# TensorE's order inside the attention units, the first shared projections, and three smaller moves in a Flamingo-style block

## The reference

```python
    x = x + jnp.tanh(g_xattn[0]) * _L0_xattn_ref(_layernorm(x, axis=-1), ctx_1024, ctx_1024, ...)
    x = x + jnp.tanh(g_ffn[0]) * _L0_ffn_ref(_layernorm(x, axis=-1), ...)
# attention: softmax(gamma * Q K^T / 4 + delta * bias) V, then Wo
# feed-forward:
        logits = xf @ gate_w + gate_b
        top_w, top_i = jax.lax.top_k(logits, K)
        for e in range(E):
            h = jax.nn.gelu(xf @ w1[e] + b1[e], approximate=False)
            out = out + combine[:, e:e + 1] * (h @ w2[e] + b2[e])
        shared = jax.nn.gelu(xf @ ws1 + bs1, approximate=False) @ ws2 + bs2
```

## Time and profile before

| what | before |
|---|---|
| median of 3 runs | 480.17 us (478.01 to 481.91) |
| the profiled execution's own time | 479.94 us |
| its span (first to last instruction) | 478.1 us |
| mean granted PE clock | 0.989 |
| PE / PEld busy | 459.8 us (96%) / 391.2 us (82%) |
| DVE / ACT / POOL busy | 357.1 (75%) / 312.7 (65%) / 244.1 us (51%) |
| PE busy, 0 to 24 us | 20.86 of 24 us |
| PE busy, 280 to 460 us | 180 of 180 us |

### The profile page before, as it was taken

One profiled execution on the slowest core, in us unless ns is written; L12 is line 12 of the kernel. 1 busy time (PEld: TensorE's weight loads), 2 busy tenths in 40 slices (PEclk: granted clock), 3 DMA queues, 4 the chain that ended last, 5 costly groups with the idle time before them and its releaser, 6 DMA issues.

```text
span 478.1 us, 17105 instructions
## 1 busy us (share of the span) xinstructions
PE 459.8 (96%) x6326; PEld 391.2 (82%) x6327; DVE 357.1 (75%) x839; ACT 312.7 (65%) x852; POOL 244.1 (51%) x277
## 2 busy tenths in 40 slices
PE   8899989999999989999999999999999999999993
PEld 4566779899999856666668999999999999999992
DVE  5897898999999966898975896566656665666562
ACT  5996788999999986878865753443344334433440
POOL 4689998998745665377850024232223222322332
PEclk9999998999999989999999999999999999999998
DMA  8704456766754377136338353423342332233223
GB/s 316 261 12 106 85 154 182 214 191 184 213 159 122 127 271 303 35 114 201 136 106 200 111 102 45 54 44 55 55 47 44 56 54 44 44 61 49 44 34 35
DMA packets 61443, 55.81 MB, mean 117 GB/s; under 512 B 37712, under 2 KB 51920, under 8 KB 61264
## 3 DMA queue, kind: packets, MB, share of 16 engines
q1 hardware_dynamic: 54240, 45.66, 33.7%
q0 software_dynamic: 7152, 9.44, 11.0%
HBM read 30.94 MB, written 19.03 MB: 105 GB/s over the span
## 4 chain that ended last, share of the span: by engine, by line
PE 69%; ACT 20%; DVE 4%; DMA 3%; issue 2%; POOL 1%; POOLq 0%; DVEq 0%; ACTq 0%
PE banks L1293 34%; PE bank L1293 32%; ACT W L750 10%; ACT W L756 5%; DMA out<-xrow,idu 2%; PE bank L1400 2%; ACT W L764 1%; ACT W L780 1%; ACT W L772 1%; PE banks L1314 1%; DMA W<-ctxT 1%; ACT xT L785 1%; DVE mx L958 0%; DVE W L963 0%; DVE gwhl L1039 0%
## 5 line engine op out<-in xcount | busy, mean ns | idle before, releaser
L886 ACT ACTIVATE hbuf<-banks,b1t 128x128 f32<-128x128 f32 x312 | 88.8, 368 | 113.3 <-PE banks L1293 110.9
L686 POOL DMA_INDIRECT out<-xrow,idu x39 | 61.0, 1564 | 167.8 <-DVE xrow L1266 128.6
L1293 PE MATMUL banks<-xrow,W 128*128 128x128 bf16 x1872 | 110.9, 219 | 0.3 <-issue 0.3
L1293 PEld LDWEIGHTS banks<-xrow,W 128*128 x1872 | 107.3, 98 | 1.8 <-issue 0.6
L1293 PE MATMUL bank<-W,xT 128*128 x936 | 108.4, 273 | 0.0
L1293 PEld LDWEIGHTS bank<-W,xT 128*128 128x128 bf16 x936 | 89.9, 98 | 9.8
L750 ACT ACTIVATE W<-banks,mx 128x128 f32<-128x128 f32 x256 | 69.6, 394 | 2.8 <-DVE mx L958 2.8
L1247 DVE TENSOR_TENSOR xT<-hbuf,xT 128x512 bf16<-128x512 f32 x78 | 54.0, 692 | 2.7
L1245 DVE CAST xT<-hbuf 128x512 bf16<-128x512 f32 x78 | 36.6, 470 | 20.1 <-ACT hbuf L886 19.3
L963 DVE TENSOR_TENSOR W<-bank,W 128x512 bf16<-128x512 f32 x64 | 43.9, 689 | 7.7 <-ACT W L756 4.9
L672 POOL DMA_INDIRECT xs_dram<-W,place x32 | 38.8, 1214 | 17.8 <-DVE W L1180 9.5
(11 more groups left out here) (175 smaller groups left out, 725.4 us busy)
## 6 DMA issues: line engine op xcount, KB each, us to landing
stage<-wts SPq DMA_DIRECT2D x26, 512.0 KB, 4.0
W<-wts SPq DMA_DIRECT2D x10, 512.0 KB, 6.5
xs_dram<-hbuf SPq DMA_DIRECT2D x6, 792.0 KB, 6.2
W<-d_dram SPq DMA_DIRECT2D x32, 128.0 KB, 3.5
W<-ctxT SPq DMA_DIRECT2D x4, 512.0 KB, 5.5
xrow<-x SPq DMA_DIRECT2D x4, 512.0 KB, 7.5
d_dram<-W SPq DMA_DIRECT2D x16, 128.0 KB, 3.9
out<-xrow SPq DMA_DIRECT2D x4, 512.0 KB, 3.5
```

Of the source, the lines that this page charges most:

```text
L686: nc.gpsimd.indirect_dma_start(out, bass.IndirectOffsetOnAxis(idu[:, par, t:t + 1], axis=0), ysb[par][t], None, compute_op=ALU.add).then_i ...
L886: ins = nc.scalar.activation(hbuf[:, q, c * TR:(c + 1) * TR], bank[UPS * par + q][:, c * TR:(c + 1) * TR], ACT.Gelu, bias=b1t[:, par, UC * ...
L1293: return nc.tensor.matmul(o, a, b, start=start, stop=stop, **kw)
```

## The change

Six parts.

1. **Units.** PE's order becomes `weigh_values(2u - 2)`, `turn_probs(2u)`, `weigh_values(2u - 1)`, then in odd units `turn_o`, `turn_probs(2u + 1)`, `turn2`, `gate`, and in even units the first 2 of `project_o`'s 8 matmuls, `turn_probs(2u + 1)`, and the other 6; then `scores(u + 2)`. Neighbours lie in different banks.
2. **Last units.** In units 30 and 31, which have no `scores(u + 2)`, PE does `shared_up(0)` and `shared_up(1)` there. ACT's order behind the units follows: the GELU table, `norm2(13)`, the GELU of step 0, `outputs_high(15)`, `inputs2_high(13)`, then `piece_high` of piece 16; that of piece 17 goes to step m = 3. On POOL `deviation2(14)` comes ahead of piece 16 and piece 17 behind the five shared splits.
3. **Beginning.** The first group's statistics, deviations and norms are made for two sequences at a time, `turn_inputs` takes each sequence as its norm is ready, and it comes after two instead of three parts of `project_values(0)`. ACT's `weight_high(0)` moves behind `norm4(0)`; the low part of the value weights moves from POOL to DVE, the selection rows `selb` from ACT to POOL.
4. **Gate weights.** `split_gate` moves from DVE (unit 3) to POOL, ahead of `clip(0)`.
5. **Last tile.** In step j = 38 PE does half 1 of `up_part(38)` behind both halves of `down_part(37)`.
6. The norms of every group release `turn_inputs` sequence by sequence.

The diff, cut to its core (`ranks`, `w_up`, `shared_up` and others only move up in the file):

```diff
-            def deviation4(g):
-                at = slice(4 * g, 4 * g + 4)
-                pool.wait_ge(ln1_moments, g + 1)
+            def deviation(n, lo, hi):
+                at = slice(lo, hi)
+                pool.wait_ge(ln1_moments, n + 1)
                 link(nc.gpsimd.tensor_tensor(rstd1[:, at], rstd1[:, at], mhalf[:, at], ALU.pow))
...
+            def split_gate():
+
+                gw = col[:, K_GW:K_GW + DC * E].rearrange("p (c e) -> p c e", c=DC)
+                nc.gpsimd.tensor_copy(upb[:], cst[:, C_UP:C_UP + P])
+                link(nc.gpsimd.tensor_copy(gwhl[:, 0], gw))
+                nc.gpsimd.tensor_tensor(gwhl[:, 1], gw, gwhl[:, 0], ALU.subtract).then_inc(gate_split, 1)
+
...
-            pool.wait_ge(w_hi, 2)
-            nc.gpsimd.tensor_tensor(wp_at(2, 1), wst_at(2), wp_at(2, 0), ALU.subtract).then_inc(w_lo[2], 1)
-            deviation4(0)
+            deviation(0, 0, 2)
+            deviation(1, 2, 4)
             pool.wait_ge(ld_cst, 16)
+            nc.gpsimd.tensor_copy(selb.rearrange("p (j t) -> p j t", t=T),
+                                  cst[:, C_SEL:C_SEL + 4 * DC].rearrange("p (j o) -> p j o", o=1).to_broadcast([P, 4 * DC, T])
+                                  ).then_inc(sel_rows, 1)
             nc.gpsimd.tensor_copy(padt[:, :, 3:4], cst[:, C_PAD:C_PAD + TH].rearrange("p (k o) -> p k o", o=1)).then_inc(pad_ready, 1)
-            deviation4(1)
...
-            deviation4(2)
+            deviation(3, 8, 12)
...
+            split_gate()
             clip(0)
             clip(1)
-            deviation4(3)
+            deviation(4, 12, 16)
...
+            deviation2(B - 2)
             piece_low(NOW // 2, 0)
-            deviation2(B - 2)
-            piece_low(NOW // 2, 1)
             deviation2(B - 1)

             for m in range(POOL_SPLITS):
                 pool.wait_ge(sh_hi, m + 1)
                 nc.gpsimd.tensor_tensor(hsplit[:, m % DEEP, 1, :], hbuf[:, m % DEEP, :], hsplit[:, m % DEEP, 0, :],
                                         ALU.subtract).then_inc(sh_ready[0], 1)
+            piece_low(NOW // 2, 1)

             pool.wait_ge(pad_written, PADS)
...
             def norm4(g):
-                act.wait_ge(ln1_rstd, g + 1)
                 if g:
+                    act.wait_ge(ln1_rstd, g + 2)
...
-            nc.scalar.activation(selb.rearrange("p (j t) -> p j t", t=T),
-                                 cst[:, C_SEL:C_SEL + 4 * DC].rearrange("p (j o) -> p j o", o=1).to_broadcast([P, 4 * DC, T]),
-                                 ACT.Copy).then_inc(sel_rows, 1)
+            norm4(0)
             weight_high(0)
-            norm4(0)
             for g in range(Q4):
...
-            act.wait_ge(converted, NOW)
-            piece_high(NOW // 2, 0)
-            act.wait_ge(setup_act, 2)
-            nc.scalar.activation(tgx[:, 1:2], tgf[:, 0:1], ACT.Gelu)
-            norm2(B - 3)
-            piece_high(NOW // 2, 1)
-            outputs_high(B - 1)
-            inputs2_high(B - 3)
...
+            act.wait_ge(setup_act, 2)
+            nc.scalar.activation(tgx[:, 1:2], tgf[:, 0:1], ACT.Gelu)
+            norm2(B - 3)
+            act.wait_ge(pad_written, PADS)
+            gelu_shared(0)
+            outputs_high(B - 1)
+            inputs2_high(B - 3)
+            act.wait_ge(converted, NOW)
+            piece_high(NOW // 2, 0)
...
+                if m == 3:
+                    piece_high(NOW // 2, 1)
...
-                if u == 3:
-                    split_gate()
...
-            statistics4(0)
+            statistics(0, 2)
+            statistics(2, 4)
+            weight_low(2, 1)
...
-            statistics4(1)
+            statistics(4, 8)
...
             def turn_inputs(g):

-                pe.wait_ge(xh_ready, g + 1)
                 if g == 0:
                     pe.wait_ge(ld_cst, 16)
-                    pe.wait_ge(sel_rows, 1)
-                for c in range(DC):
-                    if g:
-                        pe.wait_ge(xT_lo, DC * (g - 1) + c + 1)
-                    for s in range(4):
+                for s in range(4):
+                    pe.wait_ge(xh_ready, 4 * g + s + 1)
+                    for c in range(DC):
+                        if g and s == 0:
+                            pe.wait_ge(xT_lo, DC * (g - 1) + c + 1)
                         ins = nc.tensor.transpose(bank[c][:, s * T:(s + 1) * T], xh[:, s * D + c * P:s * D + (c + 1) * P], ident)
-                    ins.then_inc(xT_ps, 1)
+                        if s == 3:
+                            ins.then_inc(xT_ps, 1)
...
-            def project_o(b):
-                pe.wait_ge(oT_lo, b + 1)
...
-            project_values(0, 0, 3)
+            project_values(0, 0, 2)
             turn_inputs(0)
-            project_values(0, 3, 4)
+            project_values(0, 2, 4)
...
                     weigh_values(2 * u - 2)
+                turn_probs(2 * u)
+                if u >= 1:
                     weigh_values(2 * u - 1)
+                if u % 2 == 1 and b >= 1:
+                    turn_o(b - 1)
+                if u % 2 == 0 and b >= 2:
+                    project_o(b - 2, 0, 1)
+                turn_probs(2 * u + 1)
+                if u % 2 == 0 and b >= 2:
+                    project_o(b - 2, 1, 3)
+                if u % 2 == 1 and b >= 3:
+                    turn2(b - 3)
                 if u % 2 == 1 and b >= 4:
                     gate(b - 4, b - 3)
-                turn_probs(2 * u)
-                if u % 2 == 0 and b >= 2:
-                    project_o(b - 2)
-                if u % 2 == 1 and b >= 1:
-                    turn_o(b - 1)
-                    if b >= 3:
-                        turn2(b - 3)
-                turn_probs(2 * u + 1)
                 if u + 2 < 2 * B:
                     scores(u + 2)
+                else:
+                    piece_converted(pe, 3)
+                    shared_up(u + 2 - 2 * B)
...
-            piece_converted(pe, 3)
-            shared_up(0)
             turn_o(B - 1)
             turn2(B - 3)
-            shared_up(1)
+            shared_up(2)
             project_o(B - 1)
             turn2(B - 2)
-            for m in range(2, AHEAD):
+            for m in range(3, AHEAD):
...
+                last = isinstance(j, int) and j == TILES - 1
+                for q in range(UPS - 1 if last else UPS):
                     up_part(j, par, up_base, q)
                 if not first(j):
                     for q in range(UPS):
                         down_part(j - 1, 1 - par, down_base, q)
+                if last:
+                    up_part(j, par, up_base, UPS - 1)

```

133 lines of the change are left out of this document (69 added, 64 removed).

## The result

The changed kernel took **486.13 us** (median of 4, 485.80 to 486.61) against 479.88 for the kernel before (median of 4, 478.01 to 481.91): ratio **1.0133** (95% interval 1.0096 to 1.0170), 1.3% slower. Repeated on another chip it was 1.0147 (1.0112 to 1.0182). The forecast was 476.0 with a range of 471.5 to 480.5. The profiled execution took 486.42 us with a span of 484.6, 6.5 more than before.

What follows compares the result with a forecast made beforehand. PE was taken as full from 280 to 460 us, with time lost ahead in four places and PE, ACT and DVE near balance in attention. Terms -1.8 - 2.8 - 2.4 + 0.9 + 2.2 = -3.9 gave 476.0 us, range 471.5 to 480.5.

Steps and rivals of the forecast that it cites:

- Units: Attention pairs: ACT's waits for the second turns go, a pair falls from 7.35 to 7.24 us; -1.8 us in all.
- The slower rival: Attention: first turns hold up PE waiting for exponentials, a pair takes 7.95 us, the kernel 485.6 us; chance 0.08.
- Beginning: Program start: queries begin 1.3 us later, partly given back at `turn_inputs(1)`; +0.9 us, bounds 0 and +2.6.
- the clock falls at the beginning: Rival: a 2 us PE hole before the first queries brings the clock down; 477.5 us, chance 0.18.
- Gate weights: Units 4 to 7: moving the split off DVE removes the wait and clock fall; -2.8 us, bounds -3.2 and -1.1.
- What is late next: Behind the gate weights' split on POOL: if its cover goes, `scores(0)` is late next, by under 1 us.
- Last units: Passage to the shared expert: two shared projections fill PE's holes and avoid the half clock; -2.4 us.
- Last tile: End of the kernel: `weigh(37)` and the last adding DMAs come 2.2 us later; +2.2 us, bounds +1.9 and +2.4.
- the third rival: Attention: small PE holes bring the clock down again; 477.7 us, with a second such fall 479.4; chance 0.10.

Runs made afterwards that it cites:

- run 1: Changed kernel with `turn2(b - 3)` again right behind `turn_o(b - 1)` on PE, ahead of the second turns; ratio to the kernel before 1.0032.
- run 2: Changed kernel with ACT's `probs_high(2u + 1)` ahead of `outputs_high(b - 1)` in odd units, PE's order kept; ratio to the kernel before 1.0071.
- run 3: Changed kernel with the whole old order of PE within the units, all else still changed; ratio to the kernel before 1.0071.
- run 12: Kernel before with gate weights, difference loads, last units and late gate products: mended last tile 0.9939; old tile 0.9922; old tile plus changed beginning 0.9977.
- run 7: Kernel before with only the gate weights' split moved to POOL ahead of the first clip; ratio to the kernel before 1.0007.
- run 4: Changed kernel with PE's old order in the last tile; ratio to the kernel before 1.0076.
- run 5: Changed kernel with `weigh(37)` between the splits of the two halves on DVE in the last tile; ratio to the kernel before 1.0090.
- run 11: Kernel before, unchanged, traced again: span 476.6 us; and kernel before with the last-units part, including norms released one by one: ratio 0.9983.
- run 10: Changed kernel with units, beginning and last tile as before, keeping the gate weights and last units; ratio to the kernel before 0.9968.
- run 6: Changed kernel with the old beginning, the rest still changed; ratio to the kernel before 1.0117.

## Why the prediction was wrong

The sum said -3.9 us and the spans differ by +6.5. Of these 10.4 us, 7.8 lie in the term of the units.

**Units (-1.8, measured +6.0): the step that failed.** "The new order lets the second turns start as soon as the exponentials end, so I expect both waits gone." I looked at what the second turns wait for, and not at who waits for what had been moved behind them. `outputs_high(b - 1)` waits, through the bank that both use, for the `turn2(b - 3)` of its own unit. That took 0.66 us of ACT in each odd unit, and ACT was the full engine. Runs 1 and 2 show it from both sides, run 3 prices the order at 0.54 us per pair. The part of the term that I did look at came true: the even unit went from 3.59 to 3.45 us, the 0.14 that I had read as its wait for the second turns. The odd unit, where I had hoped for 0.11, lost 0.69. With that wait mended it still takes 4.13 and 4.17 us (runs 1 and 2), against 3.76 before: smaller waits of ACT are left (0.23 and 0.40), and the order gains nothing there. The slower rival had the size right (7.95 forecast, 7.90 measured) by luck. Its mechanism, PE's wait at the first turns, is real (0.48 us in even units), but the even unit in which it stands got shorter, and run 2 gains 0.28 of a pair with PE's order unchanged.

**Beginning (+0.9, measured +2.6).** The shift of the queries was 1.8 instead of 1.3. The rival "the clock falls at the beginning" (0.18) came true in this trace, and in five of the nine traces with that beginning: behind holes of 2.68, 2.69, 2.83, 2.84 and 2.84 us. In the four others the hole was 2.68. Against a price of 2.1 us (run 12), 0.9 left out too much. The deviation took 1.07 us beside DVE against 0.73, and DVE's L1060 1.00 beside POOL's cast, against 0.35 in the kernel before without it. The first lay on the path, the second in front of a wait. The Trainium skill's rule ("SBUF — State Buffer", the section "Who interferes with whom") that spoke against the move, by which a DVE operation with two SBUF inputs contends with one of POOL that reads SBUF, is borne out. Each lost less than it overlapped, 0.34 of 0.51 us and 0.65 of 0.86.

**Gate weights (-2.8, measured -3.2 in place).** Right in the stretch, and no part of the result: alone it gives nothing that can be measured (run 7, 1.0007). "What is late next" I had sought at `scores(0)`; it was the difference load, three engines off (POOL, SP, then the transfer). In the changed kernel's trace it had cover, because the beginning, with its fall of the clock, had made everything later. In three other traces with that beginning and no fall in it (the repeat, runs 4 and 5) the same load cost PE 0.60, 1.07 and 0.86 us.

**Last units (-2.4, measured -1.5).** Of the 3.9 us that there were to win, 1.7 were the fall of the clock, taken as a part of the old order. It is none (run 11: one trace of four has it). What was left over, 0.6, came back in part at the next GELU: 0.2.

**Last tile (+2.2, measured +2.3).** Right, by its mechanism and its size (runs 4 and 5).

That the clock would fall again in the attention by small holes, the third rival, did not happen: pairs with a PE wait of 0.48 us ran at 1.00. The Trainium skill ("TensorE: Matmul & The Clock Gate", the section "A second HAM failure mode: psum-queue depth-cycling") tells of a clock that goes up and down with small idles between groups. The pairs of the attention show none of that. Of the 20 falls in the 18 traces, those at the very end of the program aside, 15 followed a single hole of 0.97 to 2.84 us. Five followed a row of smaller ones: the one that begins with 0.65 at 168 us, and four near 225 us on the slower chip, as here in run 4:
```profile
222.88 0.71 PE L1299 MATMUL bank<-W,hsplit 128*128 128x256 bf16 x5 [0.83 <-issue]
...
224.32 0.38 PE L1299 MATMUL bank<-W,hsplit 128*128 128x256 bf16 x2 [0.73 <-issue]
```
So small idles are not harmless everywhere; where the line runs, these traces don't show.

## What to carry to other kernels

Before an instruction is moved behind another, list every wait on its semaphore, those for a shared buffer too, and see which of them belong to the engine that is full. A stall that is removed in one place is worth what the next bound lets through: follow the queue that feeds the next stage (here POOL, SP, the load) before the gain is put down. And take the times of a fall of the clock from more than one execution before a term rests on it.

## What the runs showed of the hardware

- **A fall of the clock is partly chance.** The kernel before, executed 25 times on one chip, took 476.4 to 482.0 us, with mean granted clocks of 0.995 at 476.6 and 0.985 at 481.0. The same hole, 2.68 us at the beginning, was followed by a fall in one trace and by none in four others; of the four holes of 2.69 to 2.84 us at that place, each was. A fall lasted 3.4 us at half in 17 cases and 6.8 us in three (run 10, and runs 4 and 6 on the slower chip).
- **PE stops within a group of products.** At about 90 us in 12 of 18 traces (0.5 to 1.8 us long) and at 134 to 136 in four (0.5 to 1.3), always at the same place of the program, with no wait named and no semaphore inside the group. The second place lies some 1000 matmuls behind the first (2089 to 2090 against 1089 to 1094 as the traces count them). The DMA share was 1.0 to 1.2 in the microseconds ahead of the first, also in traces without that hole. Whether it is the supply of instructions was not tried.
- **One chip was 1.5% slower for every kernel.** There the kernel before took 487.0 us. In all four traces (runs 1, 3, 4 and 6) ACT stood still for 6.3 us from a point between 213 and 218 us (row below, of run 1), and for 2.0 to 3.4 us once more some 2.4 us after it had gone on, and the clock fell behind the first of the two. None of the other chips showed this. What "remote" is stays open.
```profile
219.77 0.63 ACT L873 ACTIVATE hsplit<-hbuf 128x512 bf16<-128x512 f32 x1 [6.31 <-remote]
```
